# One expert matrix kept in SBUF, and padded keys shared between two engines, in a four-layer attention and feed-forward kernel

## The chip, the cores and the metric

The kernel runs on one core of one Trainium2 chip. The metric is the time of one execution on the device, in microseconds (us); lower is better. Five engines work side by side, each with its own instruction queue: TensorE (PE; its weight loads are shown as PEld), VectorE (DVE), ScalarE (ACT), GpSimd (POOL) and SyncE (SP), which here only issues DMA transfers. They meet through semaphores. SBUF is the on-chip memory of 128 partitions, PSUM the accumulators that TensorE writes (eight banks), and DMA engines move data between DRAM and SBUF.

## The reference

Eight sequences of 256 tokens of width 256 (2048 tokens) pass four layers, each a cross-attention to a context of 120 tokens a sequence, and a feed-forward part, both added to the tokens. Layer normalisation stands before each. The parts that the change touches are the attentions of layers 1 to 3 and the mixture of experts of layer 3:

```python
# layer 3, attention with 32 heads (layers 1 and 2: 16 heads)
scores = jnp.einsum('bqhd,bkhd->bhqk', qp, kp) / np.sqrt(dh)
attn = jax.nn.softmax(jnp.where(mask, NEG, scores), axis=-1)
y = jnp.einsum('bhqk,bkhd->bqhd', attn, vp)
# layer 3, eight experts, one chosen for each token
probs = jax.nn.softmax(x_flat @ Wg + bg, axis=-1)
assignments = jnp.argmax(probs, axis=-1)
h = jax.nn.gelu(jnp.einsum('nd,edh->neh', x_flat, W1) + b1[None], approximate=False)
eo = jnp.einsum('neh,ehd->ned', h, W2) + b2[None]
out = (w * selected).reshape(N, T, d)   # selected: eo of the chosen expert
```

## The kernel before

**Tiling.** The tokens stay in SBUF as x. A pair is two sequences, 512 tokens in four tiles of 128; there are four pairs (PAIRS). Each engine's program is written out by hand, in its own order, with semaphores between them.

**Attention.** The function attention(L) stands once for each engine. It steps through units: a unit is two heads of one sequence, 16 units a pair in layers 1 and 2 and 32 in layer 3. In each step TensorE scores a unit (L1786 to L1791), ScalarE takes the exponential (L1405) and its 16-bit high part (L1411), VectorE the low part (L931), and TensorE multiplies with the values three steps behind. Three buffers hold the exponentials. While pair i is scored, pair i+1 is prepared in the same steps: u is the step within the pair. The first pair of a layer is prepared in steps without scores.

**Keys.** Keys are split into a high and a low 16-bit part (khi, klo; L880, L884). For scoring, each part is written into a padded tile Kpad, once for each head of a group, times a mask column rm that leaves that head's partitions: 128x960 elements a copy. A layer of 16 heads needs four copies of each part (hg = 4), layer 3 needs eight. VectorE writes the high copies (padded_keys, L890), half of them in step 1 and half in step 2; ScalarE writes the low ones later (low_keys, L1391). Queries are split in the same steps: ScalarE writes high queries (L1382, L1385) for one half in step 1 and the other half in step 2, and VectorE then the low queries (L900, L904). From step 3 on TensorE forms approximate scores with the high parts (L1757 and L1759), whose maxima VectorE takes (L913). TensorE's first approximate product of a pair waits for the mask, the high copies (semaphore kpad) and the low queries (qlo). VectorE's order in steps 1 and 2 is: low part of an exponential, half of the high copies, low queries, maxima. ScalarE's is: exponential, its high part, high queries. Keys alternate between an even and an odd Kpad tile; layer 3 has its own larger ones in the same memory.

**Experts.** After the last attention each token's row (with its statistics and weight) is scattered by GpSimd to a DRAM area of its expert (L610). A table (jtab) is computed that gives for each of 23 jobs an expert and a block of 128 rows. For each job SyncE reads a register from the table (value_load) and issues job_weights (L506) into jw, one of NB = 6 buffers, and job_rows (L509) into jx. A job's weights are a kit of both expert matrices and both biases, copied together in DRAM earlier (4 DMAs for the matrices, 2 for the biases, issued at the end of layer 2's attention). Its width is KIT = 1282 floats a partition, 641 KB a job; a job's rows are 264 floats a partition, 132 KB. SyncE first issues six weight transfers, then waits until all rows are scattered (Hf.sent), then issues rows; from job 6 on it waits for the output of job j-6 and issues both. VectorE normalises the rows (L1264) and adds the second bias (L1266); TensorE transposes them (L2076), multiplies with the first matrix (job_up, L2085) and, after ScalarE's GELU (L1562), with the second (job_down, L2094); VectorE puts the output together (L1278) and GpSimd scatters it (L626). TensorE does in step j the transposes of job j, up of j-1 and down of j-2. VectorE does in step j the input of job j and then the output of job j-3.

## Time and profile before

| | us |
|---|---|
| median of 3 runs (lowest to highest) | 1650.95 (1648.97 to 1652.41) |
| the profiled execution | 1653.79 |
| its span in the trace | 1651.9 |
| TensorE busy | 1439.7 (87%) |
| VectorE busy | 1073.0 (65%) |
| ScalarE busy | 757.3 (46%) |
| GpSimd busy | 116.4 (7%) |

In order of time the span holds: layer 0 to about 311 us, attention 1 to about 500, feed-forward 1 to about 652, attention 2 to about 866, feed-forward 2 to about 1222, attention 3 to about 1543, then the routing and, from 1566, the jobs of the experts.

How to read it: a row of the timeline or of the groups tells when an engine began an instruction, how long it took, its line in the kernel, what it wrote and read, and, in brackets, how long the engine had been idle before it and what ended that. The chain of waits is followed back from the last instruction: at each step to what released it. Busy shares are averages over stages with different limits, so they are read by stretches of time. A record can overlap the next one on the same engine, so the distance of two starts is often less than one duration.

### The profile page before, as it was taken

The page shows a single profiled execution, that of the slowest core. Times are in us where ns is not written, and L with a number is a line of the kernel's source. Part 1 is how long each engine was busy: PE and PEld are TensorE (multiplying, and loading weights), DVE is VectorE, ACT ScalarE, POOL GpSimd, SP SyncE. Part 2 cuts the span into 40 slices and gives each one's busy share as a digit, 9 for nine tenths or more (in the row PEclk, how much of TensorE's full clock was granted, in tenths as well). Part 3 has the DMA queues.
Part 4 walks back from the last instruction along what each step waited for, and adds up shares of the span by engine and source line. Part 5 has one row for each costly group of instructions (what it writes and reads, how often), then busy time and mean ns, then how long its engine had stood idle before and what let it go on. Part 6 is the DMA issues. An engine that isn't in the chain of part 4 may idle for free.

```text
span 1651.9 us, 26234 instructions
## 1 busy us (share of the span) xinstructions
PE 1439.7 (87%) x9842; PEld 1075.5 (65%) x9849; DVE 1073.0 (65%) x2358; ACT 757.3 (46%) x1264; POOL 116.4 (7%) x168
## 2 busy tenths in 40 slices
PE   7999999778878995799888999999988899989356
PEld 5666666557773443477776878787854777779245
DVE  4465665778877873787746464645458988876234
ACT  2212111267773674575752222222234877788123
POOL 1000000000000000111000000000011101010413
PEclk9999999999998997999989999999999999999679
DMA  9552201410000000000009810000100000000176
GB/s 323 185 180 77 77 15 62 168 41 14 13 3 1 1 1 7 18 14 13 2 2 339 261 53 1 1 1 0 33 7 7 1 7 2 7 2 2 64 258 225
DMA packets 60269, 102.64 MB, mean 62 GB/s; under 512 B 11076, under 2 KB 48957, under 8 KB 59967
## 3 DMA queue, kind: packets, MB, share of 16 engines
q1 hardware_dynamic: 57726, 84.53, 15.6%
q10 hardware_dynamic: 544, 12.16, 2.2%
q0 software_dynamic: 1872, 4.27, 0.7%
q8 instruction: 79, 1.29, 0.3%
q14 instruction: 48, 0.39, 0.1%
HBM read 79.24 MB, written 39.40 MB: 72 GB/s over the span
## 4 chain that ended last, share of the span: by engine, by line
PE 51%; issue 18%; DVE 15%; ACT 5%; DVEq 4%; DMA 3%; SPq 1%; POOL 1%; ACTq 1%; POOLq 1%
PE bank L1989 9%; PE bank L1990 9%; PE bank L1681 7%; PE bank L1659 7%; DVE MB L913 3%; PE bank L1786 2%; DVE plo L931 2%; DMA jx<-copy_routed 2%; PE bank L1837 2%; PE bank L1587 1%; PE bank L1790 1%; PE bank L1791 1%; PE bank L1757 1%; PE bank L1759 1%; PE bank L1719 1%
## 5 line engine op out<-in xcount | busy, mean ns | idle before, releaser
L931 DVE TENSOR_TENSOR plo<-e,phi 120x512 f16<-120x512 f32 x256 | 180.2, 709 | 51.1 <-ACT phi L1411 47.4
L1405 ACT ACTIVATE e<-bank 120x512 f32<-120x512 f32 x256 | 150.9, 589 | 43.8 <-PE bank L1791 34.7
L1411 ACT ACTIVATE phi<-e 120x512 f16<-120x512 f32 x256 | 161.7, 632 | 8.7
L913 DVE TENSOR_REDUCE MB<-bank 128x4 bf16<-128x480 f32 x256 | 156.0, 649 | 13.8 <-PE bank L1759 10.6
L1336 ACT ACTIVATE act<-bank,bin 127x512 f32<-127x512 f32 x64 | 43.2, 688 | 167.2 <-DVE dec L751 163.2
L1659 PE MATMUL bank<-xT,winT 128*127 128x512 f32 (+1 forms) x256 | 114.6, 593 | 1.3 <-ACTq L1307 1.3
L1681 PE MATMUL bank<-woutT,msk 128*128 128x256 f32 (+1 forms) x512 | 115.2, 379 | 0.0
L670 DVE TENSOR_SCALAR high<-raw 128x512 int32<-128x512 int32 x96 | 41.0, 427 | 111.8 <-ACT raw L1540 60.8
L1681 PEld LDWEIGHTS bank<-woutT,msk 128*128 128x128 f32 (+1 forms) x512 | 96.9, 190 | 15.4
L1989 PE MATMUL bank<-hah,h1w 128*128 128x512 f32 x256 | 101.3, 396 | 3.6 <-DVE hal L673 3.6
L550 POOL TENSOR_TENSOR veps<-mv,ceps 128x4 f32<-128x4 f32 x32 | 8.9, 277 | 1346.1 <-DVEq L641 1214.2
L1786 PE MATMUL bank<-Q_odd,Kpad_odd 128*120 128x256 f16 x512 | 102.0, 282 | 1.1 <-ACT e L1405 1.1
L1786 PE MATMUL bank<-Q_even,Kpad_even 128*120 128x256 f16 x512 | 101.2, 280 | 1.4 <-ACT e L1405 1.3
L1990 PE MATMUL bank<-hal,h1w 128*128 128x512 f32 x256 | 100.6, 393 | 0.0
L1989 PE MATMUL bank<-hb,h2w 128*128 128x512 f32 x256 | 100.0, 391 | 0.0
L1990 PE MATMUL bank<-hbl,h2w 128*128 128x512 f32 x256 | 99.7, 389 | 0.0
L1759 PE MATMUL bank<-MB,identb 128*128 128x480 bf16 x256 | 98.1, 383 | 0.0
L1921 PE MATMUL bank<-hpad,taps 128*128 128x512 f32 x192 | 89.1, 601 | 1.0 <-ACT hc L1474 1.0
L1659 PEld LDWEIGHTS bank<-xT,winT 128*127 128x127 f32 (+1 forms) x256 | 48.3, 189 | 51.2 <-issue 49.4
L1786 PEld LDWEIGHTS bank<-Q_even,Kpad_even 128*120 128x120 f16 x512 | 64.0, 137 | 19.5 <-issue 7.0
L1757 PE MATMUL bank<-Kpad_even,Q_even 128*128 128x480 f16 x128 | 51.6, 403 | 27.6 <-DVE Q_even L904 13.3
L1790 PE MATMUL bank<-MBT_even,selm 128*120 128x256 bf16 x256 | 71.6, 280 | 0.0
(308 smaller groups left out, 3525.7 us busy)
## 6 DMA issues: line engine op xcount, KB each, us to landing
copy_routed<-zeros SPq DMA_DIRECT2D x1, 17028.0 KB
jw<-copy_experts SPq DMA_DIRECT2D x23, 641.0 KB, 5.1
seen<-in_h1T SPq DMA_DIRECT2D x8, 512.0 KB, 6.9
seen<-in_h2T SPq DMA_DIRECT2D x8, 512.0 KB, 5.1
h1w<-copy_h1T SPq DMA_DIRECT2D x1, 4096.0 KB, 17.1
h2w<-copy_h2T SPq DMA_DIRECT2D x1, 4096.0 KB, 14.2
ctxp<-in_ctxT SPq DMA_DIRECT2D x13, 240.0 KB, 2.9
jx<-copy_routed SPq DMA_DIRECT2D x23, 132.0 KB, 4.9
```

The lines of the kernel that those rows point to most:

```text
L913: dve.tensor_reduce(MB[:, t, h0 // 8, SK + h0 % 8:SK + h0 % 8 + 4], b[:, 0:4 * SK].rearrange("p (h k) -> p h k", h=4), AX.X, ALU.max).then ...
L931: dve.tensor_tensor(plo[:, g % 3, :], e32[:, g % 3, :], phi[:, g % 3, :], ALU.subtract).then_inc(s.lo, 1)
L1405: act.activation(e32[:, g % 3, :], bank[2 + g % 3][0:SK, :], ACT.Exp).then_inc(s.exp, 1)
L1411: act.activation(phi[:, g % 3, :], e32[:, g % 3, :], ACT.Copy).then_inc(s.phi, 1)
L1659: last = pe.matmul(bank[2 + 2 * (p % 2) + c][0:n, :], winT[:, k, w0:w0 + n], xT[:, k, :], start=(k == 0), stop=(k == K2 - 1))
L1681: last = pe.matmul(bank[t // 2][:, (t % 2) * D:(t % 2) * D + D], msk0[0:n, p % 2, c, tok(t)], woutT[0:n, 2 * p + c, :], start=(p == 0 and ...
L1759: pe.matmul(ps, identb[:], MB[:, t, 0, 0:SK].unsqueeze(1).broadcast_to([128, 4, SK]), start=False, stop=True).then_inc(s.ap, 1)
L1786: pe.matmul(ps, K[i % 2][:, v, r, c, b * SK:b * SK + SK], Q[i % 2][:, c, qs], start=(v == 0), stop=False)
L1790: pe.matmul(ps, selm[:], M[i % 2][:, h // 8, qs], start=False, stop=False)
L1921: last = pe.matmul(bank[2 + g % 2][:, :], taps[:, t, j, :], hpad[:, g % 3, :, j:j + S], start=(j == 0), stop=(j == 2))
L1989: pe.matmul(ps, w, hi, start=start, stop=False)
L1990: return pe.matmul(ps, w, lo, start=False, stop=stop)
```

## The change

The second expert matrix w2e leaves the kit (641 KB become 385 KB a job) and is loaded once into SBUF, as experts (16 KB a partition), in the memory of the even padded keys. Its two DMAs are issued by SyncE when all units of the last attention's third pair are scored. TensorE reads each job's expert number from the table into a register behind the job's transposes, and job_down takes its matrix from experts at that register's place. SyncE now issues weights and rows job by job; the wait for all scattered rows stands between the first job's weights and its rows. In the attentions VectorE writes the first half of the high copies, all in step 1, and ScalarE the second half, a quarter in step 1 and a quarter in step 2, each behind its high queries of that step; it waits for VectorE's half first. A new semaphore, kact, tells TensorE's first approximate product and the next split of the keys.

```diff
-W1, W2, B1, B2, KIT = 0, K2 * D, 2 * K2 * D, 2 * K2 * D + K2, 2 * K2 * D + K2 + D
+W1, B1, B2, KIT = 0, K2 * D, K2 * D + K2, K2 * D + K2 + D
...
-    assert at[0] <= r5
+    assert at[0] <= kpad_at
+    at = [kpad_at]
+    experts = put("experts", [128, NE, K2, D], F32, at)
...
-                for c, w in ((W1, "w1e"), (W2, "w2e")):
-                    for k in range(K2):
-                        sp.dma_start(kits[:, :, c + k * D:c + (k + 1) * D], a[w][:, k * 128:(k + 1) * 128, :]).then_inc(Hf.zeroed, 16)
+                for k in range(K2):
+                    sp.dma_start(kits[:, :, W1 + k * D:W1 + (k + 1) * D], a["w1e"][:, k * 128:(k + 1) * 128, :]).then_inc(Hf.zeroed, 16)
...
+        l3 = X[L3X.name]
+        sp.wait_ge(l3.sc, L3X.u0 + (PAIRS - 1) * L3X.units)
+        for k in range(K2):
+            sp.dma_start(experts[:, :, k, :], a["w2e"][:, k * 128:(k + 1) * 128, :].rearrange("e p n -> p e n")).then_inc(ld_experts, 16)
...
-        for j in range(NB):
-            job_weights(j, sp.value_load(jtab[0:1, 1, j:j + 1], min_val=0, max_val=NE - 1))
-        sp.wait_ge(Hf.sent, 16 * NT)
         for j in range(JOBS):
             if j >= NB:
                 sp.wait_ge(Hf.out, j - NB + 1)
-                job_weights(j, sp.value_load(jtab[0:1, 1, j:j + 1], min_val=0, max_val=NE - 1))
+            job_weights(j, sp.value_load(jtab[0:1, 1, j:j + 1], min_val=0, max_val=NE - 1))
+            if j == 0:
+                sp.wait_ge(Hf.sent, 16 * NT)
             job_rows(j, sp.value_load(jtab[0:1, 0, j:j + 1], min_val=0, max_val=NE * PLACES))
...
             def split_keys(j):
                 dve.wait_ge(s.k32, L.c0 + j + 1)
+                if j >= 1:
+                    dve.wait_ge(s.kact, L.c0 + j)
...
-            def padded_keys(j, part):
-                if j >= 2 and part == 0:
+            def padded_keys(j):
+                if j >= 2:
                     dve.wait_ge(s.sc, L.u0 + (j - 1) * n)
-                for r in range(part * HG // 2, (part + 1) * HG // 2):
+                for r in range(HG // 2):
                     last = dve.tensor_scalar(K[j % 2][:, 0, r, :, :], khi[:], rm[:, r:r + 1], None, ALU.mult)
-                if part == 1:
-                    dve.drain().then_inc(s.kpad, 1)
+                last.then_inc(s.kpad, 1)
...
                     if u == 1:
                         dve.drain()
-                    padded_keys(i + 1, u - 1)
+                        padded_keys(i + 1)
                     low_queries(i + 1, u - 1)
...
+            def padded_keys(j, part):
+                if part == 0:
+                    act.wait_ge(s.kpad, L.c0 + j + 1)
+                for r in range(L.hg // 2 + part * L.hg // 4, L.hg // 2 + (part + 1) * L.hg // 4):
+                    last = act.activation(K[j % 2][:, 0, r, :, :], khi[:], ACT.Copy, scale=rm[:, r:r + 1])
+                if part == 1:
+                    last.then_inc(s.kact, 1)
...
                 if ahead and u in (1, 2):
                     high_queries(i + 1, u - 1)
+                    padded_keys(i + 1, u - 1)
...
                     pe.wait_ge(s.kpad, L.c0 + j + 1)
+                    pe.wait_ge(s.kact, L.c0 + j + 1)
...
+        def job_expert(j):
+            e = pe.value_load(jtab[0:1, 1, j:j + 1], min_val=0, max_val=NE - 1)
+            return experts[:, ds(e, 1), :, :].rearrange("p o w n -> p (o w) n")
...
-        def job_down(j):
+        def job_down(j, w):
...
-                last = pe.matmul(bank[6 + j % 2][:, 0:D], jh[:, j % 3, k, :], jw[:, j % NB, W2 + k * D:W2 + (k + 1) * D], start=(k == 0),
+                last = pe.matmul(bank[6 + j % 2][:, 0:D], jh[:, j % 3, k, :], w[:, k, :], start=(k == 0),
...
+            pe.wait_ge(ld_experts, K2 * 16)
+            pe.wait_ge(Hf.tab, 1)
+            weights = []
             for j in range(JOBS + 2):
                 if j < JOBS:
                     job_transposes(j)
+                    weights.append(job_expert(j))
                 if 1 <= j <= JOBS:
                     job_up(j - 1)
                 if j >= 2:
-                    job_down(j - 2)
+                    job_down(j - 2, weights[j - 2])
```

## Rows read from the trace of the kernel before

**Rows 1.** Page, part 1: busy us (share of span), instructions of each engine.

```profile
PE 1439.7 (87%) x9842; PEld 1075.5 (65%) x9849; DVE 1073.0 (65%) x2358; ACT 757.3 (46%) x1264; POOL 116.4 (7%) x168
```

**Rows 2.** Busy time by stretches: stretch, length, engines, clock, DMA share, GB/s.

```profile
core 0: us, PE busy (x) PEld busy (x) DVE busy (x) ACT busy (x) POOL busy (x), PEclk, DMA share, GB/s
1336.00:1408.00 72.00, 66.51 (x656) 54.84 (x656) 62.46 (x126) 55.13 (x92) 4.61 (x5) 0.95 0.02 5
...
1566.00:1580.00 14.00, 0.00 (x0) 0.00 (x0) 0.00 (x0) 0.00 (x0) 0.84 (x1) 0.50 0.93 345
...
1605.00:1625.00 20.00, 14.21 (x92) 11.10 (x91) 9.63 (x35) 6.42 (x20) 6.81 (x7) 1.00 0.94 308
```

**Rows 3.** Timeline of SyncE, job stage: start, us, line, what is issued.

```profile
1566.16 6.03 SPq L506 DMA_DIRECT2D jw<-copy_experts  x6
1572.97 5.83 SPq L509 DMA_DIRECT2D jx<-copy_routed  x6
...
1590.15 0.13 SPq L509 DMA_DIRECT2D jx<-copy_routed  x1
```

**Rows 4.** Chain of waits, job stage: start, us, what the chain went through.

```profile
1601.28 4.93 DMA jx<-copy_routed
...
1609.59 4.92 DMA jx<-copy_routed
...
1636.02 5.00 DMA jx<-copy_routed
```

**Rows 5.** DMA issues by line: count, KB each, median us from issue to landing.

```profile
ctxp<-in_ctxT SPq DMA_DIRECT2D x13, 240.0 KB, 2.9
```

**Rows 6.** Tile jx, all 23 row transfers: least, median and largest landing.

```profile
DMA to landing us min/median/max: 3.5/4.9/5.0
```

**Rows 7.** Timeline of VectorE and TensorE in the jobs (jobs 0, 4, 5).

```profile
1580.26 0.41 DVE L1264 TENSOR_SCALAR jxln<-jx 128x256 f32<-128x256 f32 x1 [15.22 <-DMA jx<-copy_routed]
...
1587.60 0.48 DVE L1278 SCALAR_TENSOR_TENSOR jout<-bank,jx,jres 128x256 f32<-128x256 f32 x1 [4.07 <-PE bank L2094]
...
1589.38 0.38 PE L2076 MATMUL bank<-ident,jxln 128*128 128x128 f32 x2
...
1591.36 0.38 PE L2076 MATMUL bank<-ident,jxln 128*128 128x128 f32 x2
```

**Rows 8.** Timeline of GpSimd: the last of 16 scatters of rows.

```profile
1565.86 0.97 POOL L610 DMA_INDIRECT copy_routed<-cells,placei  x1 [0.30 <-issue]
```

**Rows 9.** Tile longw: TensorE's one register load; duration least/median/largest, start.

```profile
L2040 PEldq TENSOR_LOAD <-longw x1: 490/490/490, 862.5 to 862.5; - x1
```

**Rows 10.** Chain of waits at that time: start, us, what.

```profile
862.33 3.80 PE bank L1837 x8
```

**Rows 11.** Timeline, last attention, start of pair 1, preparing pair 2.

```profile
1338.37 1.38 ACT L1385 ACTIVATE Q_even<-bank,bias 64x512 f16<-64x512 f32 x2
...
1340.93 1.38 ACT L1385 ACTIVATE Q_even<-bank,bias 64x512 f16<-64x512 f32 x2
...
1338.13 1.61 DVE L890 TENSOR_SCALAR Kpad_even<-khi,rm 128x960 f16<-128x960 f16 x4
...
1345.29 0.56 PE L1757 MATMUL bank<-Kpad_even,Q_even 128*128 128x480 f16 x1 [2.29 <-DVE Q_even L904]
```

**Rows 12.** The same at the start of pair 0, preparing pair 1.

```profile
1273.52 1.38 ACT L1385 ACTIVATE Q_odd<-bank,bias 64x512 f16<-64x512 f32 x2
...
1277.19 0.36 PE L1757 MATMUL bank<-Kpad_odd,Q_odd 128*128 128x480 f16 x1 [2.20 <-DVE Q_odd L904]
```

**Rows 13.** The same for the layer's first keys, before any scores.

```profile
1228.86 1.61 DVE L890 TENSOR_SCALAR Kpad_even<-khi,rm 128x960 f16<-128x960 f16 x4
...
1235.42 0.56 PE L1757 MATMUL bank<-Kpad_even,Q_even 128*128 128x480 f16 x1 [6.07 <-DVE Q_even L904]
```

**Rows 14.** Line L1391, low copies on ScalarE: ns least/median/largest, first and last start.

```profile
L1391 ACT ACTIVATE Kpad_even<-klo,rm x32: 1080/1082/1097, 320.8 to 1377.1; 128x960 f16<-128x960 f16 x32
```

**Rows 15.** Timeline, first attention, start of pair 1, preparing pair 2.

```profile
390.35 1.19 ACT L1382 ACTIVATE Q_even<-bank 64x512 f16<-64x512 f32 x2
...
393.72 0.36 PE L1757 MATMUL bank<-Kpad_even,Q_even 128*128 128x480 f16 x1 [1.72 <-DVE Q_even L900]
```

More of the change, by code:

```diff
@@ L359, in build @@
         sem("h_" + n) for n in ("consts", "zeroed", "sent", "norm", "xt", "xT", "up", "act", "down", "out"))
+    ld_experts = sem("ld_experts")
     ld_job = [sem(f"ld_job{b}") for b in range(NB)]
@@ L370, in build @@
             sem(L.name + "_" + n) for n in ("mb", "ap", "red", "mt", "mbt", "sc", "exp", "phi", "lo"))
-        s.pv, s.pvc, s.o, s.klow = (sem(L.name + "_" + n) for n in ("pv", "pvc", "o", "klow"))
+        s.pv, s.pvc, s.o, s.klow, s.kact = (sem(L.name + "_" + n) for n in ("pv", "pvc", "o", "klow", "kact"))
         if L is not L1X:
@@ L393, in build @@
     W_COPIED = 5 * 16
-    ZEROED = (1 + 2 * K2 + 2) * 16
+    ZEROED = (1 + K2 + 2) * 16
     LD_L2, LD_L3X, LD_L3 = (4 + 3 + 2 * 2 + 2) * 16, 4 * 16, 2 * 16
@@ L523, in _ @@
                             (ld_l1, LD_L1), (ld_l2, LD_L2), (mask_ready, (0, 16 * 5, 16 * 9)[sum(phases > q for q in (2, 4))]),
-                            (w_copied, W_COPIED), (ld_h1, PAIRS * LD_SEEN + 64), (ld_h2, 16 if phases > 5 else 0),
+                            (w_copied, W_COPIED), (ld_h1, PAIRS * LD_SEEN + 64), (ld_h2, 16 if phases > 5 else 0), (ld_experts, K2 * 16),
                             (ld_l3x, LD_L3X if phases > 6 else 0), (ld_l3, LD_L3 if phases > 6 else 0),
```

## The prediction

> **What bounds the kernel now.** I read the table of busy time by engine first: TensorE is busy 87% of the span [rows 1], so a change pays only where TensorE waits, or where nothing on it sets the end. Then the same table by stretches, because the average hides stages with different limits. In the attention stretches TensorE, VectorE and ScalarE are all nearly full (66.5, 62.5 and 55.1 us of 72 in one pair of the last attention, clock 0.95). In the expert stage at the end it is different: from 1566 to 1580 us no engine computes at all while the DMA engines are 93% busy, and from 1605 to 1625 TensorE does 14.2 of 20 us while the DMA engines are 94% busy at 308 GB/s [rows 2]. So the job stage is bound by transfers, the attentions by the exchange between three engines. The change touches one thing in each.
>
> The chain of waits in the job stage shows how transfers bound it. SyncE may ask for job k+6 only when job k is put out, and VectorE puts out job k behind the input of job k+3; so one trip round the loop carries three jobs. One trip is the distance of two row transfers on the chain, 1609.59 - 1601.28 = 8.31 us, of which 4.93 us is the transfer's landing and 3.38 us everything else (VectorE, the register load on SyncE, the two issues) [rows 4]. From the issue of job 6's rows (1590.15) to that of job 22's (1636.02) it takes 45.87 us for 16 jobs, 2.87 us each [rows 3, 4]. TensorE could do a job in 1591.36 - 1589.38 = 1.98 us [rows 7].
>
> **Part one, the job stage.** A job's weights shrink from 641 to 385 KB, because the second matrix is read from SBUF; with its rows (132 KB) and its output (128 KB) a job moves 645 instead of 901 KB. At today's 94% share, 2.87 us a job are 2.70 us of engine time; times 645/901 that is 1.93 us. Transfers then stop being the bound. What is late next: SyncE's own issuing. It issues six weight transfers in 6.03 us, so (6.03 - 0.34)/5 = 1.14 us per issue with its register load [rows 3], two a job, 2.28 us. The loop gives nearly the same: the rows' landing is 4.9 us in the median and 3.5 at best today, and a 240 KB load lands in 2.9 us on an idle queue [rows 5, 6]. I take 3.2, nearer to the idle row because the DMA engines' share falls to some 1.93/2.28 = 85%; (3.38 + 3.2)/3 = 2.19 us. The larger, 2.28, rounded to 2.3, is my pace. Bounds: 2.2 and 2.6 (loop with a landing of 4.4).
>
> The order of issues changes too. Today six weight transfers go ahead of the first rows, which are issued at 1572.97; the first job's input starts at 1580.26 [rows 3, 7]. After, rows 0 stand right behind weights 0 (1566.16), except that SyncE waits there for all scattered rows. The last scatter is issued at 1565.86 and takes 0.97 us [rows 8]; its landing isn't shown, I bound it by 1.6 to 3.5 us and take 2.4: 1569.2. With 0.7 us of register load the rows go out at 1569.9 and land at 1573.1, 7.2 us earlier. Behind this wait stand only the other jobs' transfers, 2.28 us apart, each in time for a TensorE that starts at half clock (1.2 GHz, granted 0.50) [rows 2]: today job 0 takes 1587.60 + 0.48 - 1580.26 = 7.8 us from input to output [rows 7]; I take 8.5, since the inputs come one by one and a register load is added: output 0 at 1581.6, job 6's rows 2.07 us behind it (1590.15 - 1588.08), 1583.7, that is 6.5 us earlier than today. Sum: -6.5; 16 jobs x (2.87 - 2.30) = -9.1; the last landing 5.0 to 3.2 = -1.8; +1.0 because jobs 1 and 2 also come out slowly at half clock. **-16.4 us**, between -19 (pace 2.2, landing 2.9) and -11 (pace 2.6, landing 4.4).
>
> TensorE gets a register load per job, and a matmul operand addressed by it. Its one load today takes 0.49 us, and it starts at 862.5 us while eight matmuls begun at 862.33 still run until 866.1 [rows 9, 10]: the sequencer runs ahead of the array. In a job the load stands behind the transposes, so it delays the next matmuls by at most 0.5 us where the queue is empty, and TensorE has 2.3 - 1.98 = 0.3 us of room a job and one whole step before its result is asked for. I cost it at nothing; without that cover it is a rival below. By the Trainium skill (TensorE: Matmul & The Clock Gate, section on engine queue depths) the queue holds 64 instructions, which fits the row at 862.5; by that the load would be hidden as well.
>
> The landing price has a page too. The Trainium skill (DMA: Bandwidth & Descriptors, on the two cost components) gives a DMA about 2.0 us fixed plus its bytes over 436 GB/s: 132 KB would land in 2.3 us, an estimate below any row here (2.9 and 3.5). By it the loop would be 1.9 us, still under SyncE's 2.28, and the sum the same.
>
> The other edits have one answer. Two copies of 1 MB between DRAM areas, issued while the gated network begins, go, and two loads of 1 MB into SBUF come when pair 2 of the last attention is scored, on a queue with nothing else to do and DMA engines nearly idle; nothing waits for either. 0 us.
>
> **Part two, padded keys.** VectorE writes a padded copy in 0.40 us (four in 1.61) [rows 11]; ScalarE writes the same shape for the low halves in 1.08 us [rows 14], and I take 0.99 for one of several, since the next starts before the record of the last ends. Four (layers 1 and 2: two) of eight (four) copies move per pair. What ends last is TensorE's first approximate product of the next pair, which today waits 2.3 us for VectorE's low queries: it begins at 1345.29 [rows 11]. On VectorE 1.6 us go from the chain; on ScalarE, which also writes the high queries that these low queries need, 4 x 0.99 us come in. Replay for pair 1 to 2: high queries 0 end at 1339.75 and VectorE's half is ready at 1338.13 + 1.61 = 1339.74, so ScalarE does not wait for it; two copies, then the second high queries begin at 1342.95 instead of 1340.93, end at 1344.35, two copies to 1346.4. TensorE begins at 1346.5: **+1.2 us**. The next pair has the same pattern, +1.1. Pair 0 to 1, where the high queries come late anyway (1273.52) [rows 12]: 1273.52 + 2.0 + 1.4 + 2.05 = 1278.97, TensorE 1279.05 for 1277.19, +1.9. First keys of the layer: VectorE's half ends at 1228.86 + 1.61 = 1230.47, then 2.0 + 1.4 + 2.05 with gaps gives 1236.1 for 1235.42 [rows 13], +0.7. Last attention: **+4.9 us**.
>
> In the layers with 16 heads two copies move. Pair 1 to 2 in the first attention: high queries begin at 391.35 instead of 390.35, end at 392.55, one copy to 393.6; TensorE began at 393.72 [rows 15]: 0. The eight starts of these two layers have this pattern; where the high queries are late (pair 0 to 1) the same replay gives +0.6 twice, the two first keys -0.5 each, the others 0 to 0.1: **+0.5 us**. Behind the new work on ScalarE stand the exponentials of steps 2 and 3, 2 or 4 us later; three buffers cover about 2 us and TensorE is itself later, so I cost that at nothing; without the cover it is the slow rival. VectorE waits for TensorE rather than gaining. Attentions together **+5.4 us**. Bounds: -2 (VectorE's freed time is used later) and +10 (each last-attention start also loses 1.5 us by a longer stall and a lower granted clock, as the product at 1345.29 took 0.56 us where that at 1277.19 took 0.36 [rows 11, 12]).
>
> The Trainium skill (ScalarE: Activation LUTs, Rules for kernel authors) says to multiply on VectorE, not ScalarE, up to about three times faster in 16 bit. The rows agree, 0.40 against 0.99 us; by that rule the move costs, which has the sign of my +5.4.
>
> **Sum.** -16.4 + 5.4 = -11.0 us. The profiled execution took 1653.79 us for a span of 1651.9, 2.8 us over the median of the runs; from its own time the sum gives 1642.8, from the median 1650.95 it gives 1640.0, my forecast.
>
> **Rivals.** (a) The register load on TensorE is not hidden: 0.49 us plus some 0.2 for the address adds to 1.98, 2.70 us a job. For: the sequencer stalls behind each wait for an input. Against: [rows 9, 10]. Against today's pace 16 x 0.17 = 2.7 us are gained, with 6.5 at the start and 0.8 at the end 10.0; net -4.6: 1646. Chance 0.10. (b) The bytes are not what holds the rows: their landing stays 4.9 us, pace (3.38 + 4.9)/3 = 2.76. For: rows wait behind the weights of the same queue. Against: 94% share. -6.5 - 1.8 = -8.3, net -2.9: 1648. Chance 0.11. (c) Slower: ScalarE becomes the bound of the attentions, and each of the 32 moved copies is wholly on the path: 8 starts x 2.0 + 4 x 4.0 = +32, less 16.4: 1666. It decides once more than half of this time, 16 us, is exposed, that is when ScalarE has no idle time in the steps behind a start; today it is busy 55 of 72 us [rows 2], but in steps 4 to 7 nearly without gaps. Chance 0.06. The Trainium skill's rule on multiplying, above, points this way. (d) VectorE is the true bound of the attentions and its 32 x 0.40 = 12.8 us count half: -6.4 instead of +5.4, 1628. Against: its low queries wait for ScalarE. Chance 0.07. My own case has 0.66, by itself 1634 to 1645.
>
> **How the numbers follow.** Range 1632 to 1648: my case with its bounds, (a) and (b) are in; (c), (d) and the outer ends are left out. A measurement tells 0.2%, 3.3 us, from no change. Faster: my case nearly whole 0.64, most of (a) 0.09, some of (b) 0.04, (d) 0.07 = 0.84. Same: the rest of mine and of (a), most of (b), 0.10. Slower: (c) 0.06.
>
> **What the changed profile would show.** First job input near 1573 in today's clock (shifted by the attentions' loss); weights and rows alternating; row transfers 2.3 us apart, landing near 3.2; DMA share in the stage falling under 90%. A pace of 2.7 with TensorE's gaps before the up products speaks for (a), landings near 5 for (b). In the attentions TensorE's first approximate product waits for ScalarE instead of VectorE, 1 to 2 us later in the last one, not in the others. Wrong would make me exponentials that fall behind for a whole pair, or scattered rows landing late and holding the first job.

## The result, and the profile of the changed kernel

The changed kernel takes 1659.56 us (median of 6 runs, 1654.07 to 1660.57), the kernel before 1651.68 in the same comparison. The ratio is 1.0047, with a 95% interval from 1.0030 to 1.0065: 5 to 11 us slower, where 11 us less were predicted. The profiled execution took 1658.01 us, its span 1656.0 (before: 1653.79 and 1651.9).

Page of the changed kernel, busy us of each engine. The line that answers to [rows 1]: TensorE is 9.1 us longer busy with the same 9842 products, and ScalarE 30.6 us longer with 32 more copies.

```profile
PE 1448.8 (87%) x9842; PEld 1081.6 (65%) x9849; DVE 1061.9 (64%) x2326; ACT 787.9 (48%) x1296; POOL 116.2 (7%) x168
```

**The job stage.** SyncE's issues in the changed kernel (start, us, line, what), as [rows 3]:

```profile
1582.34 0.37 SPq L513 DMA_DIRECT2D jw<-copy_experts  x1
1586.70 0.36 SPq L516 DMA_DIRECT2D jx<-copy_routed  x1
1587.83 0.34 SPq L513 DMA_DIRECT2D jw<-copy_experts  x1
...
1600.36 0.34 SPq L516 DMA_DIRECT2D jx<-copy_routed  x1
...
1640.33 0.34 SPq L516 DMA_DIRECT2D jx<-copy_routed  x1
```

The first weights go out at 1582.34, 16.2 us later than before: that is what everything ahead lost between these two executions. From there to the end it takes 73.7 us instead of 85.7, so the stage won 12.0. Taking off the 16.2 us gives a time in the clock of before. In it job 6's rows (1600.36, so 1584.2) are 6.0 us earlier; from there to job 22's rows (1640.33) it takes 39.97 us, 2.50 a job for 2.87. The chain of waits, the first job's input on VectorE, and the landing of the row transfers ([rows 4, 6, 7]):

```profile
1581.96 3.97 DMA copy_routed<-cells,placei
...
1640.33 4.33 DMA jx<-copy_routed
```

```profile
1588.72 0.41 DVE L1271 TENSOR_SCALAR jxln<-jx 128x256 f32<-128x256 f32 x1 [7.50 <-DMA jx<-copy_routed]
```

```profile
DMA to landing us min/median/max: 2.0/3.2/4.4
```

Busy time by stretches (columns as in [rows 2]). The DMA engines move 255 GB/s instead of 308, but are still 87 to 91% busy:

```profile
1600.00:1620.00 20.00, 17.82 (x115) 14.60 (x114) 12.09 (x41) 8.18 (x25) 8.03 (x9) 1.00 0.87 255
1620.00:1640.00 20.00, 17.78 (x117) 14.98 (x118) 11.98 (x41) 8.26 (x25) 7.91 (x8) 1.00 0.91 255
```

**The last attention.** TensorE's first approximate product of each pair, as [rows 11 to 13]; behind it, the row that follows [rows 11] in the kernel before, for the last pair:

```profile
1243.22 0.56 PE L1774 MATMUL bank<-Kpad_even,Q_even 128*128 128x480 f16 x1 [7.00 <-ACT Kpad_even L1406]
...
1288.55 0.56 PE L1774 MATMUL bank<-Kpad_odd,Q_odd 128*128 128x480 f16 x1 [4.34 <-ACT Kpad_odd L1406]
...
1360.25 0.36 PE L1774 MATMUL bank<-Kpad_even,Q_even 128*128 128x480 f16 x1 [3.77 <-ACT Kpad_even L1406]
...
1433.48 0.56 PE L1774 MATMUL bank<-Kpad_odd,Q_odd 128*128 128x480 f16 x1 [3.76 <-ACT Kpad_odd L1406]
```

```profile
1417.33 0.36 PE L1757 MATMUL bank<-Kpad_odd,Q_odd 128*128 128x480 f16 x1 [2.29 <-DVE Q_odd L904]
```

The releaser is ScalarE instead of VectorE, as predicted, and the wait grew by 0.9, 2.1, 1.5 and 1.5 us. But from the first of these starts to the fourth it takes 190.26 us, where it was 1417.33 - 1235.42 = 181.91: 8.35 us more, not the 5.1 that the three longer waits between them make. What came besides stands in the stretches of 5 us behind the second start, first of before, then of the changed kernel:

```profile
1277.19:1282.19 5.00, 5.00 (x50) 4.03 (x51) 4.68 (x8) 3.97 (x7) 0.00 (x0) 1.00 0.00 0
```

```profile
1288.55:1293.55 5.00, 5.00 (x27) 3.57 (x28) 2.40 (x4) 4.33 (x7) 0.00 (x0) 0.52 0.00 0
```

TensorE is busy for all 5 us in both. Before it does 50 products at a granted clock of 1.00, now 27 at 0.52, that is nearly all at 1.2 instead of 2.4 GHz. VectorE waits for them (2.40 us busy for 4.68). Behind the third and fourth start the clock is 0.66 and 0.68; in the kernel before it is 0.70 and 1.00 there. The remaining loss lies in the other stretches: 1.0 us until the first start of layer 1, 2.5 in its attention (first to fourth start), 2.3 until the first start of layer 2, -0.3 in that attention, 2.2 until the first start of layer 3.

These rows compare one execution with one, and ahead of layer 3 that is not enough. The run e1_experts_only below has the attentions of the kernel before; its first start is also 1.2 us later, and its second attention takes 118.9 us where the kernel before took 122.4 and the changed kernel 122.1. In the profiled execution of the kernel before the granted clock fell to 0.59 and 0.72 in two stretches of that attention in which e1 has 1.00. So the -0.3 may hide a loss of some 3 us. In the last attention the two agree (181.9 and 181.7 us), and the 8.35 us stand.

### The profile page after: what moved, and what is told of

It reads as the page before. It is cut to its first block, busy times and chain, and to the rows that moved or that the text cites. A ratio compares the mean times of both kernels' runs of the same rounds, so it can differ in the third digit from the quotient of the medians.

```text
span 1656.0 us, 26359 instructions
## 1 busy us (share of the span) xinstructions
PE 1448.8 (87%) x9842; PEld 1081.6 (65%) x9849; DVE 1061.9 (64%) x2326; ACT 787.9 (48%) x1296; POOL 116.2 (7%) x168
## 4 chain that ended last, share of the span: by engine, by line
PE 53%; issue 18%; DVE 12%; ACT 7%; DVEq 4%; DMA 2%; SPq 2%; POOL 1%; ACTq 1%; POOLq 1%
PE bank L2006 9%; PE bank L2007 9%; PE bank L1697 7%; PE bank L1675 7%; PE bank L1803 3%; DVE MB L920 3%; DVE plo L938 2%; PE bank L1854 2%; PE bank L1807 1%; PE bank L1808 1%; PE bank L1774 1%; PE bank L1603 1%; PE bank L1776 1%; DMA jx<-copy_routed 1%; PE bank L1735 1%
## 5 line engine op out<-in xcount | busy, mean ns | idle before, releaser
L938 DVE TENSOR_TENSOR plo<-e,phi 120x512 f16<-120x512 f32 x256 | 179.6, 707 | 50.9 <-ACT phi L1426 47.4
L1697 PEld LDWEIGHTS bank<-woutT,msk 128*128 128x128 f32 (+1 forms) x512 | 96.9, 190 | 15.4
```

The source lines that it names most:

```text
L938: dve.tensor_tensor(plo[:, g % 3, :], e32[:, g % 3, :], phi[:, g % 3, :], ALU.subtract).then_inc(s.lo, 1)
L1697: last = pe.matmul(bank[t // 2][:, (t % 2) * D:(t % 2) * D + D], msk0[0:n, p % 2, c, tok(t)], woutT[0:n, 2 * p + c, :], start=(p == 0 and ...
```

## The experiments

Each timed kernel ran in 5 rounds beside the kernel before; ratios are against it, with 95% intervals, and 0.1% is 1.65 us. The kernel before had medians from 1649.69 to 1652.17 us in these groups, so kernels of different groups are compared by their ratios. A trace is of one execution, a ratio of several, and the two can differ by 3 to 4 us.

### The parts alone

```diff
# e1_experts_only: the change without its attention edits
# e2_keys_only: the kernel before with the attention edits alone
# e3_keys_16, e4_keys_32: the attention edits in layers 1 and 2, or in layer 3, only
...
+                if L is not L3X:        # e4: if L is L3X
                     padded_keys(i + 1, u - 1)
...
+                    if L is not L3X:
                         pe.wait_ge(s.kact, L.c0 + j + 1)
```

> The expert part of the change alone; the attentions as before. Theory A (the shares of the two traces: the job stage, from the first weight transfer to the end, took 85.7 us before and 73.7 after, everything ahead of it 16.2 us more): this kernel is 11 to 13 us faster than before, 1639 to 1641. Theory B (part of the 16 us is the one profiled execution's own scatter, or the loads of the second matrices slow the last attention): less than 8 us faster, 1644 or more.

> The padded keys shared between VectorE and ScalarE, the experts as before. Theory A: the whole loss is here, 14 to 20 us slower, 1666 to 1672, of which two thirds in the last attention. Theory B: 6 to 10 us, and the rest of the loss is in the expert part. By my prediction it would be +5.4 us, 1657.

> The sharing only in the two attentions with 16 heads (one copy moved per step). My replay said +0.5 us. The trace of after shows +2.9 in the first and +0.4 in the second of these layers. Theory A1 (a replay of starts is right, and what it lacked is the lower granted clock behind a longer stall of TensorE): +2 to +5 us, with a trace in which the clock falls behind the first starts. Theory A2 (ScalarE's whole load counts, 16 copies of 0.99 us in these layers): +12 to +16 us.

> The sharing only in the last attention with 32 heads (two copies moved per step). My replay said +4.9 us, the trace of after +9.6. Theory A1: +8 to +12 us, about 5 of it at the four starts and the rest in the stretches of lower clock behind them. Theory A2: 16 copies of 0.99 us, +16 us.

| | median us | ratio | against before |
|---|---|---|---|
| e1_experts_only | 1640.91 | 0.9925 (0.9907 to 0.9943) | -12.4 us |
| e2_keys_only | 1667.74 | 1.0101 (1.0077 to 1.0124) | +16.7 us |
| e3_keys_16 | 1657.72 | 1.0037 (1.0024 to 1.0049) | +6.1 us |
| e4_keys_32 | 1663.31 | 1.0065 (1.0047 to 1.0082) | +10.7 us |

The expert part wins less than the 16.4 predicted, but the failure is the other part: +16.7 where I had +5.4. Its halves add up to it, and the layers of 16 heads, costed at 0.5, hold 6. The expert part alone is faster than both kernels. Measured -12.4 and +16.7 make +4.3, and the whole change lies at +7.8 (5.0 to 10.7); within the intervals the parts add.

### Load, wait, or clock

The keys part does three things to the attention: 32 more copies on ScalarE, a later start for TensorE, and the clock behind it. First ScalarE's load alone:

```diff
# e5_load_split (count: a quarter of a group in step 1 and in step 2)
...
+            def spare_copies(j, part, count):
+                for r in range(part * count, part * count + count):
+                    act.activation(K[j % 2][:, 1, r, :, :], rm[:, 0:1].unsqueeze(2).broadcast_to([128, 4, 2 * SK]),
+                                   ACT.Copy, scale=rm[:, r:r + 1]).then_inc(s.kact, 1)
...
                     high_queries(i + 1, u - 1)
+                    spare_copies(i + 1, u - 1, L.hg // 4)
# e6_load_late: all of them in step 2
+                    if u == 2:
+                        spare_copies(i + 1, 0, L.hg // 2)
```

> The kernel before, VectorE and TensorE untouched; ScalarE writes in steps 1 and 2, behind its high queries, as many extra padded copies as in the change (a quarter of a group each), which nobody waits for before ScalarE's own low copies write over them. Theory A (the start of the approximate scores is late because ScalarE's copies stand ahead of the second high queries, and the longer stall of TensorE is followed by a lower granted clock): the two copies delay the second high queries by 2.0 us and with them VectorE's low queries and TensorE's start, in layer 3 by about 2.0 us, in the layers of 16 heads by up to 1.0; 1659 to 1666 us, +8 to +15 over before. Theory A2 (32 copies more on ScalarE cost their own time, wherever they stand): +12 to +17, the same as the next kernel. Theory V (VectorE's part of the exchange, or the new waits, is what costs): within 3 us of before.

> As e5_load_split, but all extra copies of a pair stand in step 2 behind the second high queries, so that they delay no query, only the exponentials behind them. Theory A: TensorE's first approximate products begin when they do in the kernel before (within 0.3 us); 1650 to 1655 us, 0 to +4. Theory A2: the same as e5_load_split, +12 to +17. If the exponentials behind are what costs, TensorE waits longer for the exponentials or low parts of steps 3 to 5, and the time lies at +5 to +12.

Measured: e5 1.0032 (1.0020 to 1.0045), e6 1.0025 (1.0012 to 1.0039), +5.3 and +4.1 us. ScalarE in e6, at the preparation of pair 2, and TensorE's start for pair 1 in e6 and e5:

```profile
1343.17 1.37 ACT L1385 ACTIVATE Q_even<-bank,bias 64x512 f16<-64x512 f32 x2
1344.58 4.05 ACT L1398 ACTIVATE Kpad_even<-rm 128x960 f16<-128x960 f32 x4
```

```profile
1279.25 0.36 PE L1764 MATMUL bank<-Kpad_odd,Q_odd 128*128 128x480 f16 x1 [2.19 <-DVE Q_odd L904]
```

```profile
1280.07 0.36 PE L1763 MATMUL bank<-Kpad_odd,Q_odd 128*128 128x480 f16 x1 [2.99 <-DVE Q_odd L904]
```

The copies are there (four in 4.05 us), the exponential behind them is 4 us late, and the whole costs 4 us in 12 preparations. So ScalarE's load, which I put at nothing, costs something, but a third or less of the 16.7. e5 was expected to delay each start by 2.0 us; it did so by 0.8 and 0.1, so theory A's size was wrong for this kernel. In the profiled executions of both the last attention takes no longer than before from first to fourth start (181.4 and 180.9 us). These two executions took 1652.75 and 1652.02 us, less than the profiled one of the kernel before (1653.79), so the traces can't show where the 4 to 5 us of the medians lie.

Next the waits of the keys part, filled with work that has no use:

```diff
# e7_keys_fill, and e16_after_fill the same on the changed kernel; e15_keys_fill_32: layer 3 only
                     pe.wait_ge(s.kpad, L.c0 + j + 1)
+                    if j >= 1:
+                        for z in range(16 if L is L3X else 8):
+                            pe.matmul(bank[7][:, :], identb[:], M[(j - 1) % 2][:, 0, :], start=True, stop=True)
                     pe.wait_ge(s.kact, L.c0 + j + 1)
```

> The keys part alone (e2_keys_only), with idle time of TensorE filled: between its wait for VectorE's half of the copies and its wait for ScalarE's, TensorE does 16 (layers of 16 heads: 8) dummy products of 128x128 by 128x512 in 16 bit into a bank that is free then, about 3.4 (1.7) us, whose result nobody reads; pairs 1 to 3 of each layer only. Theory A: the granted clock behind the starts of the last attention stays at 0.95 to 1.00 where it was 0.65 in e2_keys_only, the products there take 0.21 and 0.36 us; 1660 to 1664 us, 4 to 8 less than e2_keys_only. If the clock does not matter: within 2 us of e2_keys_only (1667.7), or above it by what the dummy products overrun.

> The keys part alone with the filled waits of e7_keys_fill in layer 3 only. e2_keys_only was at +16.7 us, e7_keys_fill at +4.6, so filling both kinds of layer is worth 12. Clock theory: layer 3, whose waits grew most (4.4 us) and whose clock fell to 0.66, holds 6 to 9 us of the 12: +8 to +11 over before. If the layers of 16 heads hold most of it: +12 to +15.

> The changed kernel whole, with the filled waits of e7_keys_fill. If the parts add up (-12.4 from the experts, +4.6 from the keys with filled waits): 1641 to 1645 us, ratio 0.994 to 0.997, faster than the kernel before where the change alone is at 1.0047. If the filling is worth less beside the expert part: 0.998 to 1.003.

| | median us | ratio | without the filling |
|---|---|---|---|
| e7_keys_fill | 1654.47 | 1.0028 (1.0016 to 1.0041) | 1.0101 |
| e15_keys_fill_32 | 1660.56 | 1.0053 (1.0036 to 1.0070) | 1.0101 |
| e16_after_fill | 1645.90 | 0.9960 (0.9948 to 0.9972) | 1.0047 |

Ninety-six useless products make the keys part 12 us faster, and the whole change 14 us: with them it is faster than the kernel before (-6.6 us, -8.6 to -4.6), near the sum of the parts (-12.4 + 4.6). The start of pair 1 in e7, and the 5 us behind it there and, before that, in e2:

```profile
1277.22 3.40 PE L1763 MATMUL bank<-MBT_even,identb 128*128 128x512 bf16 x15
1281.31 0.38 PE L1771 MATMUL bank<-Kpad_odd,Q_odd 128*128 128x480 f16 x1 [0.69 <-ACT Kpad_odd L1400]
```

```profile
1289.01:1294.01 5.00, 5.00 (x39) 4.01 (x40) 2.94 (x5) 4.24 (x8) 0.00 (x0) 0.66 0.00 0
```

```profile
1281.31:1286.31 5.00, 5.00 (x50) 4.03 (x51) 4.10 (x7) 4.89 (x8) 0.00 (x0) 1.00 0.01 3
```

From the end of its own work (1277.22) to the start it is 4.1 us, about the 4.38 of e2, for the same copies; only that TensorE is busy for 3.40 of them. The clock behind is 1.00, and it does 50 products where e2 does 39. The last attention, from its first to its fourth start, in all kernels that move its keys, and in two that do not:

| | waits of pairs 1 to 3 | granted clock in the 5 us behind each start | us |
|---|---|---|---|
| before | 2.2, 2.3, 2.3 | 1.00, 0.70, 1.00 | 181.9 |
| e1_experts_only | 2.2, 2.3, 2.3 | 1.00, 1.00, 1.00 | 181.7 |
| e7, e15, e16 (filled) | 4.2, 3.6, 3.6, filled for 3.4 to 3.6 of them | 1.00 at all nine | 185.3, 185.5, 185.3 |
| e2_keys_only | 4.4, 3.8, 3.8 | 0.66, 0.66, 0.69 | 189.0 |
| after | 4.3, 3.8, 3.8 | 0.52, 0.66, 0.68 | 190.3 |
| e4_keys_32 | 4.4, 3.8, 3.8 | 0.51, 0.50, 0.50 | 191.7 |

With the same copies on the same engines, the lower the clock behind the starts, the longer the attention. Of e2's 7.1 us over the kernel before, 3.4 are the later starts together with ScalarE's load, and 3.7 are what the filling takes away, the clock. The 5 us behind e4's start of pair 2 show the clock at its lower level throughout, with 26 products:

```profile
1352.34:1357.34 5.00, 5.00 (x26) 3.57 (x27) 3.25 (x7) 4.33 (x7) 0.00 (x0) 0.50 0.00 0
```

What does the clock take over the whole span? An estimate: TensorE's busy time in stretches of 4 us, each times one minus its granted clock, summed. That gives 50.9 us of full-speed work in the kernel before, 59.2 in e2 and 44.7 in e7. From e2 to e7 that is 14.5 less, where the time fell by 12.1. But the change itself added only the 8.3 from 50.9 to 59.2. The filling gives back more than that, because it also fills waits behind which the kernel before loses clock already.

Does a wait do this without any load on ScalarE?

```diff
# e13_stall: GpSimd, ahead of its work for pairs 1 to 3 of the last attention
+                pool.wait_ge(X["l3x"].qlo, 2 * (L3X.c0 + i) + 2)
+                for z in range(2):
+                    last = pool.tensor_tensor(junk[:, z, :], mhalf[:], mhalf[:], ALU.pow)
+                last.then_inc(late, 1)
...
                     pe.wait_ge(s.qlo, 2 * (L.c0 + j) + 2)
+                    if L is L3X and j >= 1:
+                        pe.wait_ge(late, j)
# e14_stall_fill: ten dummy products ahead of the added wait
```

> The kernel before, all its work as it is, with one thing added: in the last attention TensorE's first approximate product of pairs 1 to 3 waits, behind the low queries, for two short GpSimd operations (powers of 128x4, 1.12 us each) that begin with the low queries. TensorE's wait there grows from 2.3 to about 4.5 us, as it did in the change (4.3, 3.8, 3.8), and no other engine gets work. Clock theory: the granted clock in the 5 us behind two or three of these starts falls to 0.5 to 0.8 as in the change; +5 to +9 us, more than the wait itself shows in e7_keys_fill. Plain-delay theory: clock as before, three times at most 2.2 us: +2 to +6, and the same in e14_stall_fill. Load theory (ScalarE's work is what costs, not the wait): within 2 us of before.

> e13_stall with 10 dummy products (128x128 by 128x512 in 16 bit, 2.1 us) on TensorE between the low queries and the added wait: the start is as late as in e13_stall, but TensorE is busy for the added time. Clock theory: clock 1.00 behind the starts, 3 to 6 us less than e13_stall, at 0 to +4 over before. Plain-delay theory: the same as e13_stall.

Measured: e13 1.0069 (1.0051 to 1.0087), +11.4 us; e14 1.0048 (1.0030 to 1.0066), +7.9. Starts of pairs 1 and 3 in e13, of pair 1 in e14, and the 5 us behind pair 1's start in e13 and in e14:

```profile
1280.15 0.56 PE L1766 MATMUL bank<-Kpad_odd,Q_odd 128*128 128x480 f16 x1 [4.75 <-POOL junk L608]
...
1425.52 0.56 PE L1766 MATMUL bank<-Kpad_odd,Q_odd 128*128 128x480 f16 x1 [4.84 <-POOL junk L608]
```

```profile
1279.90 0.38 PE L1768 MATMUL bank<-Kpad_odd,Q_odd 128*128 128x480 f16 x1 [0.15 <-POOL junk L608]
```

```profile
1280.15:1285.15 5.00, 5.00 (x39) 3.81 (x40) 2.80 (x5) 1.24 (x3) 2.17 (x1) 0.66 0.00 0
```

```profile
1279.90:1284.90 5.00, 5.00 (x50) 4.03 (x51) 4.37 (x7) 2.82 (x5) 2.26 (x1) 1.00 0.00 0
```

Three waits, each 2.5 us longer, cost 11 us by the ratio with nothing added on ScalarE or VectorE, so the load theory falls for layer 3. (GpSimd's own work for these pairs begins later too; by the trace no engine waits longer for it than before.) The traces show less: the two profiled executions are 8.1 us apart, 7.7 of them in the last attention (189.7 for 181.9 us), which is hardly more than three times 2.5. The same 0.66 with 39 products as in e2 appears behind the start, and it goes away when the added time is filled. The plain delay is the larger part here: the filled kernel still loses 7.9. That the filling wins 3.5 us is what the clock theory expected, but the two intervals overlap, in the traces it wins 1.6 in the last attention (188.1 for 189.7), and this pair alone would not show it; e7 and e16 do. One of the three fillings came too late. It stands behind the 2.3 us wait for the low queries, the clock was 0.50 there from 1420 to 1423 us, and the ten dummy products took 3.95 us, so that the start came later than GpSimd's signal:

```profile
1420.02 3.95 PE L1761 MATMUL bank<-MBT_even,identb 128*128 128x512 bf16 x10 [2.28 <-DVE Q_odd L911]
```

For its size, +11.4, none of the theories was high enough.

Is it worth filling the waits as they were, too?

```diff
# e9_experts_fill: e1_experts_only with 8 (layers of 16 heads: 5) dummy products in each pair's wait
+                    pe.wait_ge(s.qlo, 2 * (L.c0 + j) + 1)
+                    if j >= 1:
+                        for z in range(8 if L is L3X else 5):
```

> The expert part alone (e1_experts_only, ratio 0.9925) with the dummy products of e7_keys_fill put where TensorE waits for VectorE's low queries at the start of each pair but the first: 8 of them in layer 3, 5 in the layers of 16 heads, behind the wait for VectorE's half-way low queries. In e1_experts_only the granted clock is 0.77 to 0.89 in 5 us behind such starts in the layers of 16 heads and 0.69 to 1.00 in layer 3. Theory A (an idle TensorE of 1 to 2 us lowers the granted clock too): 3 to 7 us less than e1_experts_only, ratio 0.988 to 0.991. If stalls of 1 to 2 us cost no clock: 0.992 to 0.995, the dummies adding their overrun.

Measured 0.9944 (0.9929 to 0.9959): not under e1's 0.9925, so it wins nothing that can be told. In the traces the clock takes 45.8 us by the sum above, 48.7 in e1. The first attention is 2.9 us shorter than e1's (110.6 for 113.5), the second 1.5 longer (120.5 for 118.9), the last 0.5 shorter. There was little to win: behind e1's starts of pairs 1 to 3 the clock is 0.71 once and 1.00 eight times. The 0.77 to 0.89 of the expectation were read from fixed stretches that did not begin at the starts.

### What sets the pace of the jobs

```diff
# e8_rows_first, on e1_experts_only; semaphores of their own for rows and weights
             job_rows(j, ...)
+            if j > 0:
+                job_weights(j, ...)
# e10_light_kit, on e1_experts_only; job_up reads one fixed matrix of experts, so the result is not the reference's
-            sp.dma_start(jw[:, j % NB, :], kits[ds(e, 1), :, :] ...)
+            sp.dma_start(jw[:, j % NB, B1:KIT], kits[ds(e, 1), :, B1:KIT] ...)
# e11_late_register, on e8_rows_first
                     job_down(j - 2, weights[j - 2])
+                if j < JOBS:
+                    weights.append(job_expert(j))
# e12_all_fill: e11 with e9's dummy products, and nine ahead of the jobs
```

> The expert part alone (e1_experts_only) with three edits in the job stage: from job 1 on SyncE issues the rows ahead of the weights; rows and weights have semaphores of their own, so that VectorE's first step of a job waits for the rows alone and TensorE's first matrix product for the weights; VectorE adds the second bias in the output step. Theory L (the round of output, two issues and the rows' landing sets the pace, 3 jobs a round): 1.1 us less in a round, pace from 2.50 to 2.2 us (SyncE's two issues are then the bound), 1634 to 1637 us, 4 to 6 less than e1_experts_only (1640.9). Theory D (the DMA engines' share of 0.89 is the bound): pace stays at 2.4 to 2.5, 1639 to 1642 us. If SyncE's issuing alone were the bound already: the pace stays at 2.5 and the landing grows.

> The expert part alone with lighter transfers: a job's kit holds only the two biases (129 KB instead of 385), and the first product of a job reads one fixed matrix of SBUF, so its result is not the reference's. A job moves 389 instead of 645 KB. Theory D (the DMA engines' share of 0.8 to 0.9 still sets the pace of 2.49 us): pace 2.2 us, where SyncE's two issues are the bound, 5 us less than e1_experts_only. Theory P (TensorE with its register load, 2.3 to 2.4 us a job, and SyncE with 2.2 set it): pace 2.35 to 2.5, within 3 us of e1_experts_only.

> e8_rows_first (ratio 0.9928, pace 2.41 us) with one edit: TensorE loads a job's register behind the second product of its step instead of behind the transposes. There its sequencer has just waited for an input and the queue is empty: the first product begins 0.6 to 0.75 us behind the transposes instead of 0.22 to 0.28. Theory P: the gap goes in nearly all jobs, TensorE's step is 2.0 us again, the pace falls to 2.2 to 2.3, 2 to 4 us less than e8_rows_first, ratio 0.990 to 0.9915. If transfers or SyncE bound e8_rows_first: no change, 0.9925 to 0.9935, and TensorE waits for the rows instead.

> e11_late_register with the dummy products of e9_experts_fill, and four and five more (128x128 by 128x512 in 32 bit, 0.9 to 1.7 us each) ahead of the jobs, where TensorE is idle from 1559.7 to 1572 us and the granted clock is 0.50. Theory A: the sum of both gains, and the jobs 0 to 2 at full clock for 1 to 2 us more: 1628 to 1634 us, ratio 0.986 to 0.989. If the gains do not add: not under 0.990.

| | median us | ratio | pace of jobs 6 to 22 |
|---|---|---|---|
| e1_experts_only | 1640.91 | 0.9925 (0.9907 to 0.9943) | 2.49 us |
| e8_rows_first | 1637.79 | 0.9928 (0.9914 to 0.9942) | 2.41 us |
| e10_light_kit | 1636.56 | 0.9912 (0.9895 to 0.9929) | 2.37 us |
| e11_late_register | 1637.88 | 0.9921 (0.9904 to 0.9938) | 2.43 us |
| e12_all_fill | 1635.68 | 0.9910 (0.9895 to 0.9925) | 2.39 us |

No ratio differs from e1's by more than the intervals, so these are read by their traces. Landing of the row transfers in e10, its stretch, and SyncE's issues there:

```profile
DMA to landing us min/median/max: 2.0/2.1/3.5
```

```profile
1583.00:1603.00 20.00, 18.39 (x127) 16.16 (x125) 12.74 (x44) 9.07 (x27) 9.01 (x9) 1.00 0.55 155
```

```profile
1599.57 0.34 SPq L516 DMA_DIRECT2D jx<-copy_routed  x1
1600.69 0.34 SPq L513 DMA_DIRECT2D jw<-copy_experts  x1
1601.80 0.34 SPq L516 DMA_DIRECT2D jx<-copy_routed  x1
```

With 389 KB a job instead of 645 the DMA engines are 55% busy and the rows land in 2.1 us instead of 3.2, yet the pace falls by 0.12 us only. SyncE's two issues take 1601.80 - 1599.57 = 2.23 us, and in e10 no two rows follow each other faster. The transfers hold 0.12 of the 0.26 us above it. In the rest SyncE waits for an output only twice, 0.6 us in all, but some of its own steps are slower: one register load took 0.49 us where most take 0.27, one issue 0.82 for 0.34. TensorE's waits in e8 and in e11 (line, us in total, times, longest):

```profile
PE bank L2102 <- issue: 2.2, 8, 0.3
```

```profile
PE bank L2088 <- DVE jxln L1275: 5.2, 5, 2.0
```

In e8 TensorE stalls 0.3 us behind the register load in 8 jobs; with the load moved this is gone, and TensorE waits for rows instead, 5.2 us. The pace stays. So the register load isn't what holds the jobs. The gains that I expected of e8, e11 and e12 did not come: by their ratios e8 and e11 are where e1 is. e12 has the lowest median and ratio of all, 1635.68 us and 0.9910, ahead of both kernels, but it is not told apart from e1 either.

## Why the prediction was wrong

**Part one, right in its mechanism, short in size.** Predicted -16.4, measured -12.4 (-15.4 to -9.4); the trace of the changed kernel gives -12.0. (The trace of e1 itself gives -9.3 for the same stage, with a last row transfer that took 5.7 us to land.) Term by term, in the clock of before: the first input was put at 1573.1 and came at 1572.5; job 6's rows at 1583.7 and came at 1584.2. The scatter's landing was 3.97 us from its issue, and I had 3.3; the first rows then landed fast enough to make up for it. The term of 16 jobs was 16 x (2.87 - 2.50) = -5.9 for -9.1: the pace was 2.50, not 2.3. I scaled the DMA engines' time with the bytes, 2.70 x 645/901 = 1.93 us, but at a share of 0.89 they are busy for 2.2 of 2.50 us, so the transfers did not get out of the way. e10 puts a size to it: with 389 KB a job the pace is 2.37, so the weights' bytes hold some 0.12 of the 0.20 that I missed. Behind job 22's rows it takes 15.7 us where it took 15.9; my -1.8 for the last landing failed, since it took 4.33 us and not 3.2. SyncE's two issues took 2.20 to 2.23 us where I had 2.28, but I took them for the pace, and no run ran at them.

**Part two, the failed step.** +5.4 predicted, +16.7 measured (12.7 to 20.5). The replay of the starts was good: in the last attention the waits grew by 0.9, 2.1, 1.5 and 1.5 where it had +0.7, 1.9, 1.2 and 1.1. What failed is that the sum made each start cost just its lateness ("TensorE begins at 1346.5: +1.2 us") and nothing for the work behind it. I had seen the sign of the clock in [rows 11, 12], the product of 0.56 us behind one wait and 0.36 behind the other, priced it at 1.5 us a start, and put it into the bounds only, and only for the last attention. The runs show in its place a loss of clock of 3.7 us over three starts in the last attention (e2 against e7), 1.2 each, near that price, and by the estimate over the span 8.3 us in all, of the 14.0 between the profiled executions of e2 and of the kernel before. The rest is 6 us by the traces and 8 by the ratio, near my +5.4, though it holds ScalarE's load, which I had put at nothing, so part of the nearness is luck. What the layers of 16 heads lose (+6.1 in e3, for 0.5) I had taken for nothing.

The second term that failed is "Behind the new work on ScalarE stand the exponentials ... I cost that at nothing". e6 has only that, and costs 4.1 us (2.0 to 6.4). The terms overlap and don't add up to 16.7. That e7, with its waits filled, is at +4.6 is not a check of my +5.4, since the filling also gives back clock that the kernel before loses.

**Two prices from outside the rows.** The Trainium skill's rule to multiply on VectorE (ScalarE: Activation LUTs, Rules for kernel authors) pointed the right way, but the ratio of the copies' times that it is about, 1.08 to 0.40 us, is not what the change paid for: e6 has the same copies for 4.1 us. The two cost components of the Trainium skill (DMA: Bandwidth & Descriptors) were fitted to transfers that GpSimd issues, while SyncE issues these; they give an estimate of 2.3 us for rows of 132 KB. e10 shows 2.1 in the median where the queue is light, and the changed kernel 3.2 where it isn't.

**The rivals.** (a) The register load was visible, 0.3 us where TensorE's queue is empty, but e11 shows that it bounds nothing. (b) Landings of 4.9 did not stay: 3.2. (c) gave the right side by the wrong mechanism: 32 copies wholly on the path would have cost 32 us; e5 and e6 price them at 4 to 5. (d) VectorE's freed time became waiting. In the last attention VectorE's maxima waited 15.0 us for TensorE, for 7.0 before (groups of VectorE from 1222 to 1500 us, last number; before, then after):

```profile
L913 DVE TENSOR_REDUCE MB<-bank 128x4 bf16<-128x480 f32 x128 | 79.2, 653 | 8.5 <-PE bank L1759 7.0
```

```profile
L920 DVE TENSOR_REDUCE MB<-bank 128x4 bf16<-128x480 f32 x128 | 79.3, 651 | 16.8 <-PE bank L1776 15.0
```

The missing rival is the one that the runs show: the longer waits of TensorE (4 us for 2 in the last attention) took the clock of the work behind them along.

**Open.** How the 12 us split between the kinds of layer: filling layer 3 alone won 7.9 us (e2 to e15), filling both 12.1, with intervals of 2 to 3 us; in the traces e7 is shorter than e2 by 4.0, 2.6 and 3.7 us in attentions 1, 2 and 3. Where ScalarE's load costs its 4 us. How much of the 16.7 is clock: 8.3 us is an estimate from one execution each, and stretches of 1 us instead of 4 would make it 10.0. Why the granted clock is lower behind one wait of 2.29 us in the kernel before and not behind the other (0.70 and 1.00); the 0.70 cost little, since the last attention took 181.9 us with it and 181.7 without it in e1.

## What to carry to other kernels

A wait of TensorE, where TensorE bounds the kernel, can cost more than its length: read the granted clock in the stretch behind each wait, price it into the sum and not only into the range, and try to fill the wait with useless products to see what it is worth. A filling can win more than the change lost, so compare it with a filled kernel before, too, ahead of calling the whole gain the cost of the change; no such run was made here. One trace per kernel is one execution: check a difference between two traces against a third with the same code. Two changes that are measured together hide each other; here the one that wins (-12.4) was outweighed by the one that loses. When a transfer shrinks, its busy time need not shrink in proportion, and the issuing queue's own time per transfer can be the next floor.

## What was unexpected of the hardware

- Behind waits of 3.8 to 4.8 us TensorE's granted clock was 0.50 to 0.69 in the next 5 us, at all twelve starts of pairs 1 to 3 in the last attention of the changed kernel, e2, e4 and e13; with the waits filled by products it was 1.00 at all twelve of e7, e14, e15 and e16 (in e14 it had been 0.50 ahead of the third). Shorter waits went either way: 2.2 to 2.3 us were followed by 1.00, 0.70 and 1.00 in the kernel before, 2.99 us in e5 by 1.00, and those at pair 1 of the first attention, 1.57 us in the kernel before and 1.72 in e1 with the same code there, by 1.00 and by 0.71.
- From the kernel before to the changed one the DMA engines' busy share fell far less than what they move: 0.94 at 308 GB/s, 0.87 to 0.91 at 255, 0.55 at 155.
- A register load on TensorE takes 0.30 us (23 of them, 296 to 489 ns) and shows as a gap of 0.3 us ahead of the next product where the queue was empty:

```profile
L2097 PEldq TENSOR_LOAD <-jtab x23: 296/300/489, 1589.3 to 1645.1; - x23
```

```profile
1604.38 0.44 PE L2093 MATMUL bank<-ident,jxln 128*128 128x128 f32 x2 [0.47 <-DVE jxln L1271]
1605.13 1.13 PE L2106 MATMUL bank<-jxT,jw 128*128 128x128 f32 x8 [0.30 <-issue]
```

- Three waits of TensorE that were 2.5 us longer, 7.6 in all, cost 11.4 us by the ratio (8.4 to 14.4) and 7.7 in the traces of the last attention: the exchange between the three engines gave nothing of the delay back.
